# TensorE multiplies an identity matrix into an unused PSUM bank at the ends of stages and in fill and drain steps

## The reference

```
for l in 0..3:
    x = x + tanh(g_xattn[l]) * attention_l(layernorm(x), ctx)
    x = x + tanh(g_ffn[l])   * ffn_l(layernorm(x))
```

## Time and profile before

| | us |
|---|---|
| median of 3 runs (2510.45 to 2514.68) | 2513.36 |
| the profiled execution, its own time | 2513.01 |
| its span, first to last instruction | 2511.2 |
| outside of the span | 1.8 |
| busy in the span: PE | 2146.8 (85%) |
| PEld | 1717.8 (68%) |
| DVE | 1787.9 (71%) |
| ACT | 1350.6 (54%) |
| POOL | 1157.7 (46%) |
| mean granted clock of TensorE | 0.915 |

### The profile page before, as it was taken

The page is one execution under the profiler, slowest core; times in us unless marked ns, Lnnn a source line. Parts: engine busy times, 40 slices in busy tenths (PEclk is TensorE's granted clock), DMA queues, the critical chain, the costliest instruction groups (busy, mean ns, idle before and its releaser), DMA issues. The chain is left out here.

```text
span 2511.2 us, 81208 instructions
## 1 busy us (share of the span) xinstructions
PE 2146.8 (85%) x33432; PEld 1717.8 (68%) x33443; DVE 1787.9 (71%) x5105; ACT 1350.6 (54%) x2499; POOL 1157.7 (46%) x1712
## 2 busy tenths in 40 slices
PE   6999999999995969999555799998399958898597
PEld 5887878787874746777444577776399947777375
DVE  3777777777773648887896589886555559988354
ACT  3555555555551327886998455553122259979232
POOL 1333333434343541113776125555466666876444
PEclk8999999999997979998677899997699979989699
DMA  6330000000005621110000111111487622332363
GB/s 194 110 123 27 25 27 25 24 21 20 20 18 152 180 85 55 55 58 17 1 1 3 32 37 52 52 51 36 134 235 230 185 75 79 106 96 79 101 185 103
DMA packets 225233, 195.14 MB, mean 78 GB/s; under 512 B 34444, under 2 KB 197846, under 8 KB 224864
## 3 DMA queue, kind: packets, MB, share of 16 engines
q1 hardware_dynamic: 186336, 143.52, 19.6%
q0 software_dynamic: 18944, 36.98, 4.2%
q10 hardware_dynamic: 19584, 9.44, 1.3%
HBM read 113.53 MB, written 70.55 MB: 73 GB/s over the span
## 5 line engine op out<-in xcount | busy, mean ns | idle before, releaser
L617 POOL DMA_INDIRECT slots<-row,put x256 | 258.1, 1008 | 211.5 <-issue 131.2
L1968 PE MATMUL experts_H<-experts_xs_t,experts_w 128*128 128x256 f32 (+1 forms) x832 | 253.5, 456 | 9.9 <-DMA experts_w<-in_F_w 4.7
L1102 ACT ACTIVATE l_prob_t<-l_banks 128x512 f32<-128x512 f32 x256 | 132.2, 603 | 145.9 <-PE l_banks L1219 115.4
L1968 PEld LDWEIGHTS experts_H<-experts_xs_t,experts_w 128*128 128x128 f32 x832 | 156.7, 195 | 74.5 <-issue 54.0
L1474 POOL TENSOR_TENSOR l_var_eps<-l_mv,eps 128x1 f32<-128x1 f32 x64 | 12.1, 189 | 413.9 <-DVE l_mv L1555 413.9
L1277 PE MATMUL l_banks<-l_val,l_prob_t 128*64 128x18 f32 x5120 | 201.1, 215 | 0.0
L1277 PEld LDWEIGHTS l_banks<-l_val,l_prob_t 128*64 128x64 f32 x5120 | 190.3, 143 | 8.1 <-issue 0.7
L1510 DVE TENSOR_REDUCE l_top<-l_S 128x16 f32<-128x1024 f32 x64 | 78.3, 1224 | 161.7 <-PE l_S L1653 161.7
L1986 PE MATMUL experts_Y<-experts_w,experts_hid 128*128 128x128 f32 x1600 | 190.0, 275 | 3.5 <-DVE experts_y L1912 2.6
L1986 PEld LDWEIGHTS experts_Y<-experts_w,experts_hid 128*128 128x128 f32 x1600 | 184.3, 192 | 5.0 <-issue 4.9
L1823 POOL DMA_INDIRECT rows<-experts_y,experts_idx x144 | 139.9, 971 | 90.0 <-DVE experts_y L1908 52.9
(11 more groups left out here) (312 smaller groups left out, 5943.4 us busy)
## 6 DMA issues: line engine op xcount, KB each, us to landing
experts_w<-in_F_w SPq DMA_DIRECT2D x136, 256.0 KB
l_ctx_t<-in_ctx_t SPq DMA_DIRECT2D x96, 128.0 KB, 2.4
early_q_m<-l_q_t SPq DMA_DIRECT2D x384, 32.0 KB, 1.8
experts_xs<-slots SPq DMA_DIRECT2D x72, 132.0 KB
experts_w<-in_F_w ACTq DMA_DIRECT2D x72, 128.0 KB, 3.3
slots<-l_empty SPq DMA_DIRECT2D x16, 536.0 KB, 4.1
experts_xs<-slots SPq DMA_DIRECT2D x16, 536.0 KB
slots<-l_empty SPq DMA_DIRECT2D x16, 520.0 KB, 5.9
```

The costliest lines, as they stand in the source:

```text
L617: pool.indirect_dma_start(self.slots, bass.IndirectOffsetOnAxis(ap=g.put[c][:, tile:tile + 1], axis=0), g.row[:, tile, self.sent_cols], No ...
L1102: nc.scalar.activation(prob_t[:, t.par(PROB), r, :], Z[:, r, :], ACT.Exp).then_inc(prob_done, 1)
L1968: last = nc.tensor.matmul(H[:, c, cols], w1_s[:, t.par(2, WS), h, c, :], xs_t[:, t.par(2), cols], start=True, stop=True)
```

## The change

A new function issues `count` matmuls of the identity with the identity (128 x 128, float32), each started and stopped by itself, into a given place of PSUM that nobody reads. They carry no semaphore. It is called

- in `attention_split`, into bank 3 of Z: at the start of the stage, before step 0 (40 in l3, 16 in l1 and l2); after each of the steps from TURN up to PROB (10 each: 4 steps in l1 and l2, 3 in l3); in l2 and l3 after each step from the one with the last OUT on (8 each, 7 steps), where the first of them comes after a wait for the last reads of that bank; and at the very end of l2 (70) and l3 (50);
- in `attention_wide`, at the very end (34), after a wait until bank 1 of R has been read for the last time;
- in `experts`, into Y at the start, ahead of the wait for `go` (14), and in experts2 after step 1 (12 more); and into X at the end (45 in experts0, 55 in experts2, none in experts3), after a wait for the last read of X.

```diff
+def keep_active(nc, g, out, count):
+    ident = g.const[:, C_IDENT:C_IDENT + P]
+    for _ in range(count):
+        nc.tensor.matmul(out, ident, ident, start=True, stop=True)
...
 # attention_split, tensor
+            IDLE = Z[:, 3, 0:P]
+            keep_active(nc, g, IDLE, 40 if head else 16)
             for t in range(FOLLOW + follower.STEPS if follower else STEPS):
                 if t == 4:
                     pe.wait_ge(ready, 1)
                 if t < STEPS:
                     step(Step(pe, ITEMS, t))
+                if TURN <= t < PROB:
+                    keep_active(nc, g, IDLE, 10)
+                if t >= ITEMS + OUT - 1 and not follower:
+                    if t == ITEMS + OUT - 1:
+                        pe.wait_ge(plus_done if stable else prob_done, 4 * ITEMS)
+                    keep_active(nc, g, IDLE, 8)
                 if following(t):
                     handed_over(t - FOLLOW)
                     follower.tensor(pe, t - FOLLOW)
             if weigh:
                 weigh.tensor(nc, pe)
+            if not follower:
+                keep_active(nc, g, IDLE, 70 if weigh else 50)
...
 # attention_wide, tensor
             pipeline(pe, ITEMS, DEPTH + 5, step, UNROLL)
+            pe.wait_ge(drained["k1"], ITEMS)
+            keep_active(nc, g, R[:, 1, 0:P], 34)
...
 # experts
-    dynamic, gated = kind == "silu", kind == "relu"
+    dynamic, gated, end = kind == "silu", kind == "relu", last
...
 # experts, tensor
                 if early:
                     early.tensor(pe, t.t)
+                if dynamic and t.t == 1:
+                    keep_active(nc, g, Y[:, 0:P], 12)
+
+            keep_active(nc, g, Y[:, 0:P], 14)
             pe.wait_ge(go, 1)
             pipeline(pe, ITEMS, DEPTH, both)
+            if not end:
+                pe.wait_ge(xt_drained, ITEMS)
+                keep_active(nc, g, X[:, 0:P], 55 if dynamic else 45)
```

## The result

| | us |
|---|---|
| kernel before, 16 runs of the same session, median | 2510.55 |
| changed kernel, 16 runs, median (2507.85 to 2533.78) | 2518.8 |
| ratio, 95% interval | 1.0042 [1.0024, 1.006] |
| the profiled execution of the changed kernel, its own time | 2514.53 |
| its span | 2512.7 |

The change makes the kernel slower: 8 us by the medians, 0.42% by the ratio. (The ratios in this document lie near those of the means and can differ from those of the medians by about 0.1%.) The forecast was 2504.4 us, 9 us faster, with a range of 2495 to 2514 us; the result has the other sign and is outside the range.

What follows compares the result with a forecast made beforehand. Half-clock stretches, mostly at stage boundaries, were taken as the target, only work ending a wait counting. Terms -5.5 (l1), -4.0 (l2), -1.5 (experts0), +1.0 and +1.0 (drains) gave -9.0 us: 2504.4 against the median, range 2495 to 2514.

Steps and rivals of the forecast that it cites:

- the price of one added matmul: All 602 added products: 0.12 us each at full clock, 0.23 at half; 72 us or 138 us of TensorE in all.
- Runs fit into 56.7 us of idle: Ahead of the experts stages' first turns: 228 products, 52 us if all at half clock, fit idle time; cost 0.
- 45 end at 916.6, before SP starts at 919.68.: End of experts0: its 45 products finish before SP starts l1, so the meeting of the engines is not delayed; cost 0.
- l1's fill step 5.9 us: Fill of l1: step shrinks from 7.04 to 5.9 us, ten new matmuls adding 1.2; 5.5 us gained in all.
- the sign of being wrong that the prediction had named: l1's fill: forecast wrong if line 1210 starts at 2.0 us, or is 1.1 with the step still 7 us.
- ten matmuls lie beside that spread and cost nothing.: Fill of l2: blocks lie beside DVE's spread of maxima and cost nothing; 4.0 us gained, bounds -1 and 5.
- experts0 -1.5: Start of experts0: first product 3.70 us instead of 5.85, next item waits for ACT; 1.5 gained, bounds 0 and 2.1.
- experts2 0, experts3 0: Starts of experts2 (clock down again after weight wait) and experts3 (run ends long before stage): gain 0; bounds 3 and 2.
- Drains +1.0 each: Drains of l2 and l3: eight matmuls exceed gaps of 0.66 and 0.78 us at half clock; 1.0 us lost each.
- rival (c): Fills and drains: clock does not rise, in-step blocks at 0.23 exceed idle; 12 us slower, 2525.5; chance 0.07.
- Rival (a): l1 and l2 fills: ACT's copies, loads or GpSimd bind; less than half of 9.5 us remains, 2509 to 2514; chance 0.23.
- Rival (b): All runs end so long before real work that the clock falls again; cost and gain 0, 2513.4; chance 0.04.

Runs made afterwards that it cites:

- the fitted version: Changed kernel without wide-end, split-end and drain blocks, 5 per fill step, shorter experts-end (27/22) and split-start (10/8) runs: 2497.93 us, repeated 2503.76 us.
- the in-step blocks: Changed kernel with only the blocks in fill steps (10) and drain steps (8), all other counts 0: 2515.89 us, ratio 1.0016.

## Why the prediction was wrong

**The step that failed is the price of one added matmul.** The prediction read 32 instructions of 3.81 us as 32 products and took 0.12 us for one product. They were 16 products: in the kernel's source line 1986 issues 16 float32 products, and the row says x32. The price of one added product is 0.24 us at full clock (ten in 2.40) and 0.45 at half (ten in 4.47 in the version with fill blocks alone), twice the forecast. Most of what else failed follows from it. Between the forecast's -9.0 and the boundary sum of +7.9, 9.0 us lie in the first two fills, 6.4 in the handovers to l1 and l3, 2.7 ahead of experts0 and 1.0 in experts0; the drains, l3's fill, experts2 and experts3 together give 2.2 back. Of this, 1.4 ahead of experts0 and 1.8 in l1's x loads are not explained by the price. Step by step:

- *Runs fit into 56.7 us of idle* (228 products at 0.23 = 52). At half clock, as the prediction priced them, they are 103, at full clock 55. Ahead of experts0 the run of 34 still ends before the stage does, and what is late there is the scatter ahead of it by 1.0 to 1.4 us, cause open.
- *45 end at 916.6, before SP starts at 919.68.* They end at 922.37 and SP starts at 922.76. Cost 2.0 to l1 and 2.3 to l3, forecast 0. The prediction named this meeting as the place to look and had the cover right (8.5 us); a doubled price would have given 45 x 0.24 = 10.8 us against it.
- *l1's fill step 5.9 us.* The chain to the block's start was forecast at 4.7 us and took 4.5 (935.78 to 940.30, 929.09 to 933.62). Then 1.2 us was to be added and 2.4 was: 6.9 us in the version with fill blocks alone. With five products, so at the forecast's price, 6.1. In the changed kernel the clock had fallen for part of the block (3.48 us), and the step is 7.9 us (935.78 to 943.71) with the scores at 1.12: the sign of being wrong that the prediction had named. The mechanism was right and the term behind it was mis-sized. Gained 0.8 in the changed kernel for 5.5 forecast, and 0.1 with the blocks alone.
- *l2: "ten matmuls lie beside that spread and cost nothing."* The place was right: the block is issued behind the small product and ahead of the scores that wait for the spread. The size was wrong: 2.4 us at best and 4.1 at worst, in 1.65 of idle, where 1.2 would have fitted, and five products of 1.33 us did, with 0.48 us to spare. +0.3 for -4.0 in the changed kernel, +2.9 with the blocks alone.
- *experts0 -1.5.* -0.5 in the changed kernel; but the mechanism holds and was sized too low. With start runs only, the first product takes 3.70 us and the stage gains 3.0, since the second item then waits only 0.93 us for ACT. I forecast that ACT would give part back, and the upper bound of 2.1 was too low.
- *experts2 0, experts3 0.* -1.3 and -0.4 in the changed kernel, so within the bounds; the fitted version shows 5 and 3 to be had.
- *Drains +1.0 each.* About 1.2 in l3 and 0.5 in l2 by the profiles, so right in sign and near in size, partly by luck: the forecast had the clock at its lower level there, and in those windows it was 0.81 and 0.87, while each product cost twice as much. l3's fill 0: right, 23.0 and 23.1.

**The rivals.** The sign was that of rival (c), at 0.07: slower because blocks exceed the idle time of the step. Its arithmetic (what exceeds the idle is lost) is what happened; its condition was not. It asked for a clock that does not rise, and the clock rose, 0.96 in l1's window; with the true price the blocks exceed the idle at full clock too. Rival (a), fills bound elsewhere, is out for five products (3 us gained in each of two fills). Rival (b), nothing kept, is right in one place, the end runs by themselves: 5.00 us of idle after them, and l1's fill as slow as before (36.6 against 35.3).

The clock rule of the Trainium skill, "TensorE: Matmul & The Clock Gate", section "HAM oscillation", which prices a stretch at the lower clock by its length, gave 2405 us. The mean granted clock rose from 0.915 to 0.950 in these runs and the time rose by 0.42%: the trace speaks against it here. The section's own example counts 1.67 us of cold time per K-tile, where matmuls run, and not the wait for DMAs beside it, so the 2405, which price the waits too, are its widest reading. For the fitted version that reading gives about 38 us, an estimate: the mean clock of 0.930 for 0.915 is 75 us less at the lower level, priced at half. It gained 8 to 13 us at the median, and no version gained more.

**The chances.** 0.66 for faster leaned on one figure for all 602 products. A cost term that multiplies everything should have had a bound of its own; both readings of x32, 32 products or 16, could have been priced, and the source would have settled it: line 1986 stands in a loop of 16.

## What to carry to other kernels

Count instructions against the source before taking a duration per product from a row: the x of the trace counts instructions, and a float32 product of 128 x 128 was two. Filler stands in the engine's stream between real products, so it has to be priced against the idle time at the very place where it is issued, at the clock it will meet there, and adjoining runs as one chain: here 10 products per fill step lost and 5 gained. A higher mean clock is no result; the fitted version has 0.930 and is faster than the changed kernel with 0.950.

## What the runs showed that was not expected

- The time that filler takes decided, not its count, as far as these runs tell: 90 float32 and 180 bf16 instructions both took 10.21 us, and the kernels with 1204 and 2408 of them had ratios of 1.0042 and 1.0032.
- The same fill blocks did not do the same in each execution. Blocks of 1.33 us held the full clock through both score products of l1's fill in one of three profiled executions, blocks of 0.72 us in neither of two.
- The time of one execution to the next varies by more than any effect here (2496.85 to 2524.5 in runs of the kernel before), and the profiles put it into the steady parts of l2 and l3, 313.5 to 322.4 and 276.8 to 293.9 us, whatever the change. Judging such a change by one span would have given +1.5 us for the changed kernel and -3.6 for the in-step blocks, one with the wrong size and one with the wrong sign. The boundary sums and the differences of medians agree within 1.5 us in eight of thirteen kernels and in sign in twelve; in the other five they are 3 to 7 us apart, so a boundary sum of one profile is evidence for a mechanism and not a measurement either.
